# Row sums on ScalarE's accumulator and two chunks of columns turned by VectorE in a stack of four graph layers

## The reference

```python
h = relu(layernorm(x))
x = x + L0(h, adj)        # e from h and small weights; LN(adj @ (adj.T @ e)) * gamma + beta + h
h = relu(layernorm(x))
x = x + adj @ h
h = relu(layernorm(x))
x = x + L2(h, adj)        # out = h@w0 + (adj@h)@w1 + ...; two more products with adj
h = relu(layernorm(x))
x = x + L3(h, adj)        # a = adj + I; degree = sum(a, axis=1); d = degree ** -0.5
                          # relu(d[:, None] * a * d[None, :] @ (h @ W + b))
```

## Time and profile before

| | |
|---|---|
| median of 3 runs | 1458.09 us (1457.35 to 1459.07) |
| profiled execution, first to last instruction | 1456.2 us |
| busy: TensorE / VectorE / ScalarE | 1422.6 / 665.2 / 226.3 us |
| DMA | 523 MB, mean 359 GB/s |
| granted TensorE clock, mean | 0.997 |

### The profile page before, as it was taken

The page is one execution under the profiler, slowest core; times in us unless marked ns, Lnnn a source line. Parts: engine busy times, 40 slices in busy tenths (PEclk is TensorE's granted clock), DMA queues, the critical chain, the costliest instruction groups (busy, mean ns, idle before and its releaser), DMA issues.

```text
span 1456.2 us, 18041 instructions
## 1 busy us (share of the span) xinstructions
PE 1422.6 (98%) x7601; PEld 601.7 (41%) x7601; DVE 665.2 (46%) x1136; ACT 226.3 (16%) x453; POOL 84.3 (6%) x67
## 2 busy tenths in 40 slices
PE   6998999999999999999999999999999999999998
PEld 3553555555555554333333333333333333333332
DVE  6699999999998734320221311011311021101044
ACT  2331423333233342000000000000000000000000
POOL 2300000000000028100000000000000000000000
PEclk9999999999999999999999999999999999999999
DMA  9998999999999998999996897989797848996998
GB/s 325 386 379 354 406 415 418 411 419 413 412 416 368 381 418 324 421 421 420 420 420 211 323 354 298 359 323 315 300 348 263 302 179 362 392 380 228 354 415 321
DMA packets 97604, 523.23 MB, mean 359 GB/s; under 512 B 18764, under 2 KB 18804, under 8 KB 54644
## 3 DMA queue, kind: packets, MB, share of 16 engines
q1 hardware_dynamic: 90436, 520.40, 91.1%
q10 hardware_dynamic: 7088, 1.67, 0.5%
HBM read 415.88 MB, written 106.17 MB: 359 GB/s over the span
## 4 chain that ended last, share of the span: by engine, by line
PE 61%; DMA 2%; DVE 1%; POOL 0%; issue 0%; ACT 0%; DVEq 0%
PE turned L630 33%; PE acc L630 25%; DMA over_wide<-adj_t 2%; PE turned L663 1%; PE turned L815 1%; PE t_rows L799 0%; PE turned L821 0%; DVE staged L1143 0%; PE t_acc L789 0%; PE t_acc L715 0%; PE t_rows L715 0%; POOL rstd L1246 0%; DVE staged L1001 0%; DVE X L1189 0%; DVE staged L1205 0%
## 5 line engine op out<-in xcount | busy, mean ns | idle before, releaser
L1016 DVE TENSOR_REDUCE deg_part<-raw 128x4 f32<-128x3072 f32 (+1 forms) x70 | 220.8, 3196 | 0.9
L641 PE MATMUL t_acc<-raw,E 128*64 128x384 f32 (+1 forms) x1120 | 187.2, 483 | 10.8 <-DMA raw<-in_adj_dram 10.7
L1105 DVE STREAM_TRANSPOSE staged<-raw 32x256 f32<-32x256 f32 x448 | 195.1, 436 | 5.8
L869 ACT ACTIVATE staged<-turned 128x512 f32<-128x512 f32 x303 | 152.7, 640 | 240.8 <-PE turned L663 240.4
L630 PE MATMUL acc<-staged,t_cur 128*64 128x512 f32 x720 | 161.1, 597 | 0.0
L663 PEld LDWEIGHTS turned<-ident,raw 128*128 128x128 f32 x1376 | 150.1, 141 | 25.5 <-issue 25.5
L663 PE MATMUL turned<-ident,raw 128*128 128x128 f32 x1376 | 160.5, 275 | 0.0
L630 PE MATMUL turned<-over_last,C 128*64 128x512 f32 x672 | 152.1, 592 | 0.0
L641 PEld LDWEIGHTS t_acc<-raw,E 128*64 128x64 f32 x1120 | 79.4, 139 | 115.4 <-issue 89.2
L1246 POOL TENSOR_TENSOR rstd<-rstd,minus_half 128x8 f32<-128x8 f32 (+1 forms) x30 | 44.2, 1474 | 1279.6 <-DVE rstd L1007 1279.6
L630 PE MATMUL turned<-over_last,R 128*64 128x512 f32 x512 | 116.5, 593 | 0.0
(11 more groups left out here) (137 smaller groups left out, 893.6 us busy)
## 6 DMA issues: line engine op xcount, KB each, us to landing
over_last<-adj_t SPq DMA_DIRECT2D x181, 1024.0 KB, 8.9
staged<-adj_t SPq DMA_DIRECT2D x91, 1024.0 KB, 9.7
raw<-in_adj_dram SPq DMA_DIRECT2D x60, 1536.0 KB, 18.4
adj_t<-staged SPq DMA_DIRECT2D x30, 3072.0 KB, 17.1
over_wide<-adj_t SPq DMA_DIRECT2D x23, 1024.0 KB, 7.1
raw<-in_adj_dram SPq DMA_DIRECT2D x10, 1024.0 KB, 15.0
adj_t<-over_last SPq DMA_DIRECT2D x8, 1024.0 KB, 12.2
adj_t<-C SPq DMA_DIRECT2D x2, 1024.0 KB, 21.7
```

Of the source, the lines that this page charges most:

```text
L641: last = nc.tensor.matmul(t_acc[h * D:(h + 1) * D, 0:columns], E[:, m * SUB + a, :], raw_of(g, m)[:, a, h * columns:(h + 1) * columns], st ...
L869: nc.scalar.activation(turned_into(g, u)[:, i * B:(i + 1) * B], turned[n % TURN_BANKS][:, :], ACT.Copy) \
L1016: nc.vector.tensor_reduce(deg_part[:, of(m), g], raw_of(g, m), AX.X, ALU.add).then_inc(deg_summed, 1)
L1105: last = nc.vector.transpose(dst[b * SQ:(b + 1) * SQ, :, :, q * SQ:(q + 1) * SQ], src[q * SQ:(q + 1) * SQ, :, :, c * P + b * SQ:c * P + (b ...
```

## The change

The row sums of groups 0 to 5, except the four at the start, 56 of 70, move from VectorE to ScalarE: one ACTIVATE copies 128 rows of a raw block (768 columns) to a place that nobody reads (`passed`, a part of `t_t` seen as bytes) and lets the accumulator write their sums to `deg_part`; a block takes four. They stand behind the copies of a pair's banks. A second semaphore, `act_summed`, counts them, and the waits for a sum choose between the two. `copy_t`, which writes `t_t`, waits for the sums so far. The sums of group 6 stay on VectorE, beside the four at the start. VectorE now turns two chunks (`VECTOR_CHUNKS`) of each pair from the third on, in groups 0 to 5, with 32 instructions, and TensorE has 8 banks (32 transposes) instead of 10. `turned_into`, `wait_turned` and all later passes are as before.

```diff
--- before.py
+++ after.py
@@ -34,6 +34,7 @@
 PASSES = 5
 MOVED_BANK = 3
 VECTOR_FROM, VECTOR_LAST = 2, 0
+VECTOR_CHUNKS = 2
 EARLY_SLOTS = 1
 LATE_SLOTS = 4
 SLOTS = EARLY_SLOTS + NB + LATE_SLOTS
@@ -267,6 +268,7 @@
         w0123 = sb("w0123", [P, 4, D])
         w3 = sb("w3", [P, 2 * D])
         ident = sb("ident", [P, P])
+        passed = [t_t[:, i * GW // 4:(i + 1) * GW // 4].bitcast(mybir.dt.uint8) for i in range(2)]
         centring = sb("centring", [P, P])
         room = staged[:, 2 * STAGE_WORDS - 4 * B:2 * STAGE_WORDS].rearrange("p (i a d) -> p i a d", i=4, d=D)
         cen = [room[:, i] for i in range(2)]
@@ -458,7 +461,7 @@
 
         def banks(g, m):
 
-            return range(2 * chunks(g) - 2 * by_vector(g, m))
+            return range(2 * chunks(g) - 2 * VECTOR_CHUNKS * by_vector(g, m))
 
         def is_moved(g, m, j):
@@ -501,11 +504,18 @@
             behind = [(g + 1, 2 * i - 2 + j) for j in range(2)] if i >= 1 else [(g, NB - 2 + j) for j in range(2)]
             return [x for x in ahead if x[1] < NB] + [x for x in behind if 0 < x[0] < NG]
 
-        SUMS = [(0, m) for m in range(SUMS_AHEAD)]
-        for g in range(NG):
-            for i in range(ROWS):
-                SUMS += sums_of(g, i)
+        PAIR_SUMS = [x for g in range(NG) for i in range(ROWS) for x in sums_of(g, i)]
+        SUMS = [(0, m) for m in range(SUMS_AHEAD)] + [x for x in PAIR_SUMS if x[0] == NG - 1]
         SUM_NO = {x: i + 1 for i, x in enumerate(SUMS)}
+        ACT_SUMS = [x for x in PAIR_SUMS if x[0] < NG - 1]
+        ACT_SUM_NO = {x: SUB * (i + 1) for i, x in enumerate(ACT_SUMS)}
+
+        def wait_summed(eng, g, m):
+
+            if (g, m) in SUM_NO:
+                eng.wait_ge(deg_summed, SUM_NO[g, m])
+            else:
+                eng.wait_ge(act_summed, ACT_SUM_NO[g, m])
 
         def of(m):
             return slice(m * SUB, (m + 1) * SUB)
@@ -567,7 +577,7 @@
             def load_next(g, m):
 
                 wait_turned(sp, g, m // 2)
-                sp.wait_ge(deg_summed, SUM_NO[g, m])
+                wait_summed(sp, g, m)
                 src = adj_v[:, m, :, (g + 1) * GW:(g + 1) * GW + chunks(g + 1) * P]
                 sp.dma_start(raw_of(g + 1, m), src).then_inc(raw_in[m], 16)
@@ -609,7 +619,7 @@
             for u in range(2, UNITS):
                 if u == UNITS - 1:
                     wait_turned(sp, NG - 1, u // 2)
-                    sp.wait_ge(deg_summed, SUM_NO[NG - 1, u])
+                    wait_summed(sp, NG - 1, u)
                     for n in first:
                         first_load(n)
                 store_kept(u)
@@ -859,7 +869,7 @@
                     u, i = 2 * m + j // chunks(g), j % chunks(g)
                     act.wait_ge(chunk_turned, n + 1)
                     if i == 0 and g == NG - 1:
-                        act.wait_ge(deg_summed, SUM_NO[g, u - 2] if u >= 2 else SUM_NO[g - 1, NB - 1])
+                        wait_summed(act, *((g, u - 2) if u >= 2 else (g - 1, NB - 1)))
                         if u < 2 and by_vector(g - 1, ROWS - 1):
                             act.wait_ge(vector_turned, VECTOR_NO[g - 1, ROWS - 1])
                         if u >= 2 and by_vector(g, m - 1):
@@ -899,8 +909,19 @@
                 act.wait_ge(t_done, g + 1)
                 if g > 0:
                     act.wait_ge(t_turned, g)
+                    act.wait_ge(act_summed, SUB * len([x for k in range(g) for i in range(ROWS) for x in sums_of(k, i) if x in ACT_SUM_NO]))
                 columns = chunks(g) * P // 2
                 nc.scalar.activation(t_t[:, 0:columns], t_acc[:, 0:columns], ACT.Copy).then_inc(t_copied, 1)
+
+            def sum_rows(g, m):
+
+                act.wait_ge(raw_in[m], g * 16 + 16)
+                for a in range(SUB):
+                    n = ACT_SUM_NO[g, m] - SUB + a
+                    if n >= 2:
+                        act.wait_ge(act_summed, n - 1)
+                    nc.scalar.activation(passed[n % 2], raw_of(g, m)[:, a, :], ACT.Copy,
+                                         accum_out=deg_part[:, m * SUB + a, g:g + 1]).then_inc(act_summed, 1)
 
             def take_t(g):
                 act.wait_ge(t_turned, g + 1)
@@ -936,6 +957,9 @@
                     if i == 0:
                         take_t(g)
                     copy_banks(*after, banks(*after)[TURN_BANKS:])
+                    for x in sums_of(g, i):
+                        if x in ACT_SUM_NO:
+                            sum_rows(*x)
 
             def last_group():
                 g = NG - 1
@@ -1096,14 +1120,16 @@
                         wait_turned(dve, g, m - 1)
                     else:
                         wait_turned(dve, g - 1, ROWS - 1)
-                    half, c = chunks(g) // 2, chunks(g) - 1
+                    half = chunks(g) // 2
                     rows = raw_flat if g < NG - 1 else raw_flat[:, 0:NB * SUB * CHUNKS_LAST * P]
                     src = rows[:, :].rearrange("p (m a h k) -> p m h a k", m=ROWS, h=2, k=chunks(g) * P)[:, m]
-                    dst = turned_into(g, 2 * m + 1)[:, (half - 1) * PAIR:half * PAIR].rearrange("p (h a n) -> p h a n", h=2, a=SUB)
-                    for q in range(4):
-                        for b in range(4):
-                            last = nc.vector.transpose(dst[b * SQ:(b + 1) * SQ, :, :, q * SQ:(q + 1) * SQ],
-                                                       src[q * SQ:(q + 1) * SQ, :, :, c * P + b * SQ:c * P + (b + 1) * SQ])
+                    for c in range(half - VECTOR_CHUNKS, half):
+                        dst = turned_into(g, 2 * m + 1)[:, c * PAIR:(c + 1) * PAIR].rearrange("p (h a n) -> p h a n", h=2, a=SUB)
+                        for q in range(4):
+                            for b in range(4):
+                                k = (half + c) * P + b * SQ
+                                last = nc.vector.transpose(dst[b * SQ:(b + 1) * SQ, :, :, q * SQ:(q + 1) * SQ],
+                                                           src[q * SQ:(q + 1) * SQ, :, :, k:k + SQ])
                     last.then_inc(vector_turned, 1)
 
             def group(g):
@@ -1112,7 +1138,8 @@
                     move_bank(*after)
                     turn_chunk(*after)
                     for x in sums_of(g, i):
-                        sum_rows(*x)
+                        if x in SUM_NO:
+                            sum_rows(*x)
                     add_h(g, i)
 
             def last_group():
@@ -1129,7 +1156,8 @@
                 group(g)
             dve.wait_ge(late_in, 16 * 8)
             last_group()
-            dve.wait_ge(deg_summed, NG * NB)
+            dve.wait_ge(deg_summed, len(SUMS))
+            dve.wait_ge(act_summed, SUB * len(ACT_SUMS))
             nc.vector.tensor_reduce(dis[:, :], deg_part[:, :, :], AX.X, ALU.add).then_inc(deg_ready, 1)
 
             def turn_squares(r):
```

More of the change, by code:

```diff
@@ L332, in gnn_stack @@
         deg_summed = sem("deg_summed")
+        act_summed = sem("act_summed")
         h_added = sem("h_added")
```

## The result

The changed kernel takes **1489.43 us** (median of 4 runs, 1487.87 to 1491.64) against 1457.72 (4 runs, 1455.7 to 1459.07): ratio 1.0215 [1.0202, 1.0227]. That is slower, as forecast, but by 32 us instead of 18, and 4 us above the range. The profiled execution, the slowest of the four, has a span of 1489.8.

What follows compares the result with a forecast made beforehand. TensorE, VectorE and the load/store queue were taken to bind within 1 us of each other, coupled through the sync queue. Layer 0's 15.5 us delay plus 2.6 for the clock gave 1474.3, predicted as a 1476.2 us median; range 1461 to 1485.

Steps and rivals of the forecast that it cites:

- T(0,2): Group 0, the first moment when VectorE has turned its part of a pair: forecast at 85.3 us.
- T(1,0): End of VectorE's turn of group 1's first pair: 132.0 us against 134.1 before, with 0.3 allowed for ScalarE's sums.
- T(1,0) to T(5,1), 21 pairs: Groups 1 to 4, at 15.65 us a pair: 328.7 us against 317.4 before.
- T(5,2) to T(5,4): Group 5: two pairs of 19.5 us, as the last group's sums stand beside 32 transposes on VectorE.
- delay of the last load: End of layer 0: load (6,9) lands at 532.5 instead of 517.0, 15.5 us later, passed through in full.
- the clock: A half product at half clock after TensorE's wait of some 8 us before the last load: 2.6 us, once.
- L: Time from a burst's issue to its last load's landing: taken as 20.2 us, between 19.7 (empty queue) and 23.2 (full).
- 26.73: Microseconds from a burst's landing to T three pairs on: half t product, turns, h product, add and VectorE's transposes.
- The loop itself: Late T delays loads, TensorE and VectorE's next turn: 3 pitches = L + 26.73, giving 15.65 us a pair.
- Rival 3: TensorE's clock falls in every pair, not once: 1.0 us a pair, 22 more, 1498 us; chance 0.05.
- Rival 4: ScalarE's sums cost 1.30 us each, so T(1,0) comes 18 us later: 1494 us; chance 0.05.
- Rivals 1 and 2: 1: TensorE binds, 1432.3 us, faster side 0.08 together. 2: queue stays fed at 15.16 a pair, 1462.8 us, 0.12.

Runs made afterwards that it cites:

- store_first: The changed kernel, but SyncE issues the store of a pair ahead of both loads instead of between them: 1467.08 us.
- filler_ahead: One chunk on VectorE with the sums on ScalarE, plus about 7 us of unused VectorE work ahead of each pair's turn in groups 0 to 4: 1476.13 us.
- turns_between: The changed kernel, but TensorE makes the 32 turns, in four of five pairs, between the halves of the t product instead of behind it: 1487.54 us.
- no_scalar_sums: The changed kernel without the 56 sums on ScalarE, which no engine then makes: 1492.24 us in one run.
- last_sums_scalar: The changed kernel with eight more sums, those of group 6 made beside group 5, moved from VectorE to ScalarE: 1477.42 us in one run.

## Why the prediction was right in sign and wrong in size

The forecast's own steps, as ends of the runs of transposes on VectorE:

| step | forecast | measured | error |
|---|---|---|---|
| T(0,2) | 85.3 | 84.7 | -0.6 |
| T(1,0) | 132.0 | 133.3 | +1.3 |
| T(1,0) to T(5,1), 21 pairs | 328.7 | 341.9 | **+13.2** |
| T(5,1) to T(5,2) | 15.6 | 18.1 | +2.5 |
| T(5,2) to T(5,4) | 39.0 | 38.8 | -0.2 |
| T(5,4) to the last load | 17.2 | 17.7 | +0.5 |
| delay of the last load | 15.5 | 32.75 | +17.3 |
| growth of the span beyond that delay (forecast: the clock) | 2.6 | 0.85 | -1.75 |
| span | 1474.3 | 1489.8 | +15.5 |

**The step that failed** is the size of L: "At 15.5 the queue can be neither empty (it needs 15.16) nor full; I take L = 20.2, nearer the empty end: 15.65 us a pair". It took for granted that a queue which is fed later still works at its full rate. Late bursts start slowly (306 to 361 GB/s around their start), so that L was a lead of 4.9 plus a burst of 16.3, 21.25 on average, and the pitch was 16.28, near my upper bound of 16.6. In the formula this L is worth 0.35 us a pair, 7.4 of the 13.2 us.

**The rest, some 5.8 us, is what the sum put at nothing.** Over the 19 turns of the loop from T(1,0) to T(5,1), the T of three pairs on stands 0.07 to 1.77 us behind T + L + 26.73, 0.82 on average and 15.6 in all. The four turns with a fall of the clock in them have 1.41 to 1.77, together 6.7; most of the others over 0.5 have a wait of VectorE for a store. In store_first, with neither, the same difference is 0.07 to 0.09 in most turns. The 2.5 us of T(5,2) have a wait of 3.01 us for a load in them, a half product at the lower clock (4.20 us) and a wait for a store of 1.11.

**The loop itself held**: T late, loads late, TensorE's wait in most pairs, the transposes' 14.37, filler_ahead's 16.19. What it lacked was its twin through the store, 15.97 with the same L, so that taking the turns out of the first alone (turns_between) was worth nothing.

**Rival 3 came true in part.** The granted clock fell to 0.50 five times between T(1,0) and T(5,1) and once more before T(5,2), behind waits of 2.0 to 3.1 us; the prediction had set waits of 1.6 us beside the wait of 0.98 that was harmless. Each fall made a half t product 1.3 to 1.7 us longer. The Trainium skill's "TensorE: Matmul & The Clock Gate", section "HAM oscillation", describes a kernel whose clock the wait before every tile throttles; here it was 4 of the 18 waits between 140 and 450 us.

**ScalarE.** A sum starts 0.825 us after the last, where I took 0.75:

```profile
324.22 0.90 ACT L923 ACTIVATE t_t<-raw 128x768 uint8<-128x768 f32 x1
324.95 0.26 ACT L923 ACTIVATION_READ_ACCUMULATOR t_t<-raw 128x1 f32 x1
325.04 0.90 ACT L923 ACTIVATE t_t<-raw 128x768 uint8<-128x768 f32 x1
```

Beside 15 us that is nothing, but in pairs 1 and 2 of group 0 TensorE waited 2.33 and 1.61 us for the copies behind sixteen sums, where I had allowed 0.3: the 1.3 us at T(1,0), which no_scalar_sums reaches at 132.0. Rival 4, with 1.30 us a sum, fell.

**Group 5** came as forecast, 19.4 a pair and 17.7 to the last load; it cost some 12 us (last_sums_scalar, one run), which is over a third of the whole loss. Rivals 1 and 2 fell: a burst landed 21.25 us behind its issue, not within 15.4, and the queue didn't keep its rate.

## What to carry to other kernels

Where an engine's last act in a step releases the next loads, moving work behind or ahead of that act matters more than how much work it is: 7.2 us ahead of it cost 20 us, behind it none. Close the loop from the issue through the landing and back for every buffer that the step frees, loads and stores both, and don't expect gains where two loops are equally long. And when transfers are issued late, try which of them goes first: moving the store ahead of both loads, one line, brought back 22 of 32 us.

## What the runs showed that I had not expected

- A load that finds the queue empty starts slowly. Of the one issued at 493.39 the first packet begins 1.05 us behind the start of the issue, 0.68 behind its end. The Trainium skill's "DMA: Bandwidth & Descriptors", section "Latency and other measured facts", gives some 0.6 us to the first byte on this path, near to that. The time is lost behind it: the 233 GB/s above, against 433 a little later.
- The way from issue to landing differs by kind of transfer. The shortest of a late load of 1.57 MB was 8.8 us in the change between 150 and 450 us (7.7 in last_sums_scalar); for a half store of the same 1.57 MB it was 6.6. Why a load behind a half store, issued 6 to 10 us ahead, still lost 1 us, where the first loads of the kernel before did not at 6 us, stays open.
- A wait of only 2.05 us was followed by half the clock, while one of 2.14 us a pair earlier was not; in filler_ahead waits of up to 2.61 us passed between 22 and 465 us without a fall.
- The accumulator's read is an instruction of its own, 247 ns, and hides under the next ACTIVATE: 768 columns with a sum run at 0.825 us apiece, against 3.3 us for a whole block of four such rows on VectorE, so 0.83: ScalarE is no slower at it.
